# Scores in each group's own bank pair, and the small PE jobs last in each attention step

## The reference

```python
x = L0_attn_x                                             # (1, 2048, 128)
h = _layernorm(x)
Q, K, V = h @ Wq + bq, h @ Wk + bk, h @ Wv + bv           # 16 heads of 64
Qp, Kp = relu(Q), relu(K)
Qc, Qs, Kc, Ks = Qp * cos(t), Qp * sin(t), Kp * cos(t), Kp * sin(t)
# over tokens: S += k v^T, z += k (cos and sin parts)
num = Qc @ S_cos + Qs @ S_sin
den = max(Qc . z_cos + Qs . z_sin, 1e-6)
x = x + (num / den) @ Wo + bo
xf = _layernorm(x)
top_w, top_idx = top_k(xf @ gate_w, 2); top_w = softmax(top_w)
y = gelu(xf @ w1[e] + b1[e]) @ w2[e] + b2[e]              # for the two experts of a token
x = x + sum of y weighted by top_w
```

## Time and profile before

| | us |
|---|---|
| median of 3 runs | 374.67 |
| lowest and highest | 371.89, 378.90 |
| the profiled execution: its own time | 376.67 |
| its span, from the first to the last instruction | 374.8 |

### The profile page before, as it was taken

The page is one execution under the profiler, slowest core; times in us unless marked ns, Lnnn a source line. Parts: engine busy times, 40 slices in busy tenths (PEclk is TensorE's granted clock), DMA queues, the critical chain, the costliest instruction groups (busy, mean ns, idle before and its releaser), DMA issues.

```text
span 374.8 us, 14556 instructions
## 1 busy us (share of the span) xinstructions
PE 334.9 (89%) x5821; PEld 301.5 (80%) x5821; DVE 240.9 (64%) x837; ACT 171.5 (46%) x449; POOL 130.5 (35%) x130
## 2 busy tenths in 40 slices
PE   7998978999999999989989998898998999999910
PEld 6776967888798888879978887887888899999910
DVE  4889846648887745888855588876557544454415
ACT  3773432457433454733443663244334455555600
POOL 5022331203008820301872020274307775445430
PEclk9999988999999999999999999999999999999985
DMA  7940622233000100000110006113635676776138
GB/s 253 306 198 2 258 90 86 99 126 134 3 7 26 57 3 2 0 2 14 35 42 2 2 1 177 54 44 99 166 97 175 177 227 190 207 189 173 33 88 250
DMA packets 32786, 38.36 MB, mean 102 GB/s; under 512 B 6187, under 2 KB 25024, under 8 KB 31696
## 3 DMA queue, kind: packets, MB, share of 16 engines
q1 hardware_dynamic: 27248, 31.39, 27.1%
q0 software_dynamic: 2272, 4.46, 3.5%
q10 hardware_dynamic: 3200, 1.58, 1.4%
HBM read 22.40 MB, written 15.47 MB: 101 GB/s over the span
## 4 chain that ended last, share of the span: by engine, by line
PE 70%; DVE 14%; issue 6%; DMA 3%; POOL 3%; ACT 1%; SPq 1%; DVEq 0%; ACTq 0%; POOLq 0%
PE ps L1399 9%; PE ps L1384 8%; PE ps L1269 8%; PE ps L1196 7%; PE ps L1210 6%; PE ps L1076 5%; PE ps L1078 5%; PE ps L1077 5%; PE ps L1223 4%; PE ps L1173 3%; PE ps L1246 3%; PE ps L1123 2%; DVE vcs L729 2%; DVE vb L725 2%; DMA zin<-zbuf 2%
## 5 line engine op out<-in xcount | busy, mean ns | idle before, releaser
L620 ACT ACTIVATE os<-ps,rot 128x130 f32<-128x130 f32 x128 | 40.3, 366 | 81.7 <-PE ps L1223 81.7
L448 POOL TENSOR_TENSOR on<-tcs,rden 128x1024 f32<-128x1024 f32 x16 | 30.5, 1904 | 102.5 <-DVE rden L802 102.4
L655 ACT ACTIVATE hT<-ps,b1t 128x128 f32<-128x128 f32 x156 | 44.5, 368 | 40.3 <-PE ps L1384 40.3
L522 POOL DMA_INDIRECT zbuf<-z,tokens x39 | 37.9, 972 | 29.4 <-DVE z L1017 25.0
L1223 PE MATMUL ps<-vcs,am 64*64 64x65 f32 x1024 | 43.9, 232 | 2.0 <-issue 0.7
L1196 PE MATMUL ps<-vcs,kn 64*64 64x130 f32 x1024 | 44.5, 287 | 1.1 <-DVE tcs L792 0.5
L1399 PE MATMUL ps<-w_sb,hT 128*128 x312 | 43.1, 282 | 1.1 <-issue 0.6
L777 DVE TENSOR_TENSOR mid<-ps,state 128x260 f32<-128x260 f32 x64 | 26.7, 417 | 26.4 <-PE ps L1196 26.1
L1399 PEld LDWEIGHTS ps<-w_sb,hT 128*128 128x128 f32 x312 | 37.8, 192 | 2.4 <-issue 2.0
L725 DVE TENSOR_TENSOR vb<-ps,bv_all 128x512 f32<-128x512 f32 x32 | 22.0, 689 | 27.2 <-PE ps L1078 27.2
L1223 PEld LDWEIGHTS ps<-vcs,am 64*64 64x64 f32 x1024 | 33.0, 136 | 4.7 <-PE ps L1223 2.8
(11 more groups left out here) (126 smaller groups left out, 662.3 us busy)
## 6 DMA issues: line engine op xcount, KB each, us to landing
ybuf<-spare SPq DMA_DIRECT2D x8, 1152.0 KB, 5.0
w1b<-in_L_ffn_w SPq DMA_DIRECT2D x25, 256.0 KB, 2.7
spare<-in_L_ffn_w SPq DMA_DIRECT2D x14, 256.0 KB
yb<-ybuf SPq DMA_DIRECT2D x39, 72.0 KB, 2.4
w_sb<-in_L_ffn_w SPq DMA_DIRECT2D x8, 256.0 KB, 4.2
x_sb<-in_L_attn_x SPq DMA_DIRECT2D x4, 256.0 KB, 5.0
zin<-zbuf SPq DMA_DIRECT2D x4, 256.0 KB, 5.1
zin<-zbuf ACTq DMA_DIRECT2D x4, 256.0 KB, 5.7
```

The source lines that it names most:

```text
L522: pool.indirect_dma_start(zbuf, bass.IndirectOffsetOnAxis(ap=tokens[:, b:b + 1], axis=0), z[:, b % ZR, :], None, bounds_check=2 * T - 1, o ...
L620: last = act.activation(os[:, n % 2, :, q, :], ps[:, slot(n):slot(n) + 2, CS + q * VW:CS + q * VW + VW], ACT.Copy, scale=rot[:, 4 + q, c:c ...
L655: act.activation(hT[:, b % 2, f, :], ps[:, b % 2 * 2 + f // 2, f % 2 * P:f % 2 * P + P], ACT.Gelu, bias=b1t[:, b % XR, f:f + 1]).then_inc( ...
```

## The change

Scores of a group go into columns 260 to 387 of the group's own bank pair instead of banks 0 and 1. They are computed one group ahead instead of two, and DVE masks each group by itself, as the first thing in its step. The wait for a free bank pair moves from the key-value products to the scores, which are now the first to write there. Banks 0 and 1 become free for small jobs, which stand last in each PE step, in a new function `fill`: the transposes of K for chunks 1 to 3 (16 transposes of 64 rows in place of two times four of 128), whole turns of chunks 0, 1 and 2, the projections of chunks 0 and 1, `turn_y`, `gate`, `ranks`, the transposes of the next section's x, and the first two blocks of the next section. The fronts keep 14 blocks (16 in the first section), V in two banks in turn, K's transposes of chunk 0, the projection of chunk 2 and the turn and projection of chunk 3; blocks go through banks 4 to 7. ACT's copies and DVE's reads of all these move along. At the start of the experts some steps change places (`turn_y`, `gate`, the turn and projection of chunk 3 one place earlier or later).

```diff
+SCORES = 2 * CS
+V_AT = ({2: 0, 4: 1, 6: 2, 8: 3, 10: 4, 12: 5, 13: 6, 14: 7}, {2: 0, 3: 1, 5: 2, 6: 3, 8: 4, 9: 5, 11: 6, 12: 7})
+OPEN_AT = (14, 13)
+OT_AT, WO_AT, KEYS_0_AT = 6, 8, 10
+STATS_AFTER = 4
+YT_AT, GATE_AT, RANKS_AT, BEFORE_AT, TABLE_AT, TURN_X_AT = 0, 2, 4, 7, 11, 11
+KEYS_AT = {1: 1, 6: 2, 10: 3}
+TURN_AT = {8: 0, 13: 1, 16: 2}
+SUMS_AT = {9: 0, 14: 1}
...
             def scores(i, n):
...
-                if n >= 2:
-                    pe.wait_ge(am_ok, i * PAIRS + p)
...
+                if n >= 3:
+                    pe.wait_ge(tcs_ok, i * GROUPS + n - 2)
                 for q in range(2):
-                    of = 2 * g + q
-                    at = of % (PH // 2) * HT
+                    of, at = 2 * g + q, SCORES + q * HT
...
             def key_values(i, n):
...
-                if n >= 3:
-                    pe.wait_ge(tcs_ok, i * GROUPS + n - 2)
...
-            def group(i, n):
-
-                if n < GROUPS:
+            def group(i, n, tail):
+
+                if 1 <= n < GROUPS:
                     key_values(i, n)
                 if n >= 1:
                     from_state(i, n - 1, 0)
                     from_state(i, n - 1, 1)
                     within(i, n - 1, 0)
-                if n + 2 < GROUPS:
-                    scores(i, n + 2)
+                if n + 1 < GROUPS:
+                    scores(i, n + 1)
                 if n >= 1:
                     within(i, n - 1, 1)
+                fill(i, n, tail)
...
+            def masked(i, n):
+
+                c = n // NG
+                if n % NG == 0:
                     dve.wait_ge(pair_in[c], i * 16 + 16)
-                dve.wait_ge(sc_ps, i * PAIRS + p + 1)
...
+                dve.wait_ge(kv_ps, i * GROUPS + n + 1)
...
                 for n in range(GROUPS):
...
+                    masked(i, n)
                     half_state(i, n)
                     if n >= 2:
                         taken(i, n - 2)
                     whole_state(i, n)
-                    if n % 2 == 1 and n // 2 + 1 < PAIRS:
-                        masked(i, n // 2 + 1)
...
             def attention(i, tail):
+                fill(i, 0, tail)
+                fill(i, 1, tail)
                 for n in range(GROUPS):
+                    if n == GROUPS - 1 and i + 1 < NS:
+                        block(i + 1, 0)
+                        block(i + 1, 1)
                     sums_out(i, n)
...
+                    fill(i, n + 2, tail)
```

More of the change, by code:

```diff
@@ L572, in turn_out @@
-            def turn_out(i, c):
+            def turn_out(i, c, bank):
                 act.wait_ge(oT_ps, 2 * (i * SC + c) + 2)
                 for half, spots in ((0, slice(0, 4, 3)), (1, slice(1, 3))):
-                    act.activation(turned(c)[:, :, spots, :], ps[:, 6 + half, :].rearrange("p (g q l) -> p g q l", q=2, l=HT),
+                    act.activation(turned(c)[:, :, spots, :], ps[:, bank + half, :].rearrange("p (g q l) -> p g q l", q=2, l=HT),
                                    ACT.Copy).then_inc(oT_ok, 1)
-            def front(i, tail):
[L580 to L592, removed]
@@ new lines, in keys, with block @@
+            def keys(i, c, bank):
+                for r in range(2):
+                    act.wait_ge(kn_ps, i * K_JOBS + 2 * c + r + 1)
+                    act.activation(kn[:, c, :].rearrange("p (b r d) -> p b r d", r=2, d=DH)[:, :, r, :],
+                                   ps[:, bank + r, :].rearrange("p (b d) -> p b d", d=DH), ACT.Copy).then_inc(kn_ok, 1)
+            def block(i, j):
+                dst = (kT if j < NP else qT)[:, j % NP, :]
+                col = (NP if j < NP else 0) + j % NP
+                act.wait_ge(big_ps, i * QK_JOBS + j + 1)
+                act.activation(dst, ps[:, 4 + j % 4, :], ACT.Relu, bias=bcols[:, col:col + 1]).then_inc(big_ok, 1)
@@ L593, in front @@
+            def front(i, tail):
+                for j in range(2 if tail else 0, QK_JOBS):
+                    block(i, j)
                     if tail and j == OT_AT:
[L594 to L597, removed]
+                        turn_out(i - 1, SC - 1, 2)
+                    if j == KEYS_0_AT:
+                        keys(i, 0, 2)
             def y_turned(u, bank):
@@ L877, in shares, with places @@
                 dve.tensor_scalar(wts[:, 1, :], th[:, here], -0.5, 0.5, ALU.mult, ALU.add).then_inc(wts_ok, 1)
-            def places(u, bank=6, at=0):
+            def places(u, bank):
                 cs = UNITS[u][1]
@@ new lines, in block @@
+            def block(i, j):
+                if j == 0:
+                    pe.wait_ge(xThi_ok, i + 1)
+                    pe.wait_ge(xTlo_ok, i + 1)
+                    if i >= 1:
+                        pe.wait_ge(tcs_ok, i * GROUPS - 2)
+                if j == 2 and i >= 1:
+                    pe.wait_ge(tcs_ok, i * GROUPS - 1)
+                if j >= 4:
+                    pe.wait_ge(big_ok, i * QK_JOBS + j - 3)
+                if i == 0 and j == NP:
+                    pe.wait_ge(whi_ok, 3)
+                    pe.wait_ge(wlo_ok, 3)
+                w, b = 1 if j < NP else 0, j % NP
+                split3(ps[:, 4 + j % 4, :], (w_hi[w], w_lo[w]), (xT_hi, xT_lo),
+                       lambda t: t[:, b * P:(b + 1) * P], lambda t: t[:]).then_inc(big_ps, 1)
@@ new lines, in keys @@
+            def keys(i, c, bank):
+                for pr in range(NP):
+                    for r in range(2):
+                        rows = slice(HT * r, HT * r + HT)
+                        last = pe.transpose(ps[:, bank + r, pr * DH:pr * DH + DH], kT[rows, pr, c * P:(c + 1) * P],
+                                            ident[rows, rows])
+                        if pr == NP - 1:
+                            last.then_inc(kn_ps, 1)
+            def front(i, tail):
+                if tail:
+                    project(i - 1, SC - 2)
+                for j in range(2 if tail else 0, QK_JOBS):
+                    block(i, j)
+                    if j in V_AT[tail]:
+                        values(i, V_AT[tail][j])
+                    if tail and j == OT_AT:
+                        pe.wait_ge(tcs_ok, i * GROUPS)
+                        turn_out(i - 1, SC - 1, 2)
@@ L1277, in turn_y, with gate @@
                 last.then_inc(yT_ps, 1)
-            def gate(u, bank=7):
+            def gate(u, bank):
                 pe.wait_ge(yT_ok, u + 1)
```

369 lines of the change are left out of this document (169 added, 200 removed).

## The result

The changed kernel takes 416.73 us (median of four runs, 416.27 to 417.65), the kernel before 375.57 in the runs beside it. The ratio is 1.1135, with a 95% interval from 1.1046 to 1.1225: slower, near the forecast of 424 and inside its range. The ratio leaves out one of the four runs of the kernel before (378.90 us), which was in the slower of its two states, and so it lies a little above the quotient of the two medians, 1.1096. The profiled execution took 416.29 us, with a span of 414.5.

The account below looks back on a forecast made before the run. PE was taken to bound the kernel. The terms summed to +49.6 us on the profiled 376.67, 426.3; that execution being 2.0 us above the median, the forecast was 424 us against 374.67, range 400 to 452.

Parts of the forecast that it names:

- The wait at the scores: Mid-step in the attentions, PE waits for DVE's `taken` before scores: step 2.41 us instead of 1.56, 52 times, +44.2 us.
- ACT's copies ahead of the scaling: In attention steps with K's transposes or turns, two ACT copies delay the next group's scaling: 20 x 0.45, +9.0 us.
- The small jobs fill none of the wait: At each step's end, jobs stand behind the waiting scores, lie on the loop in full and fill none of 0.85 us.
- The start of the attentions: PE's 1.04 us idle at each attention's start is covered by work now inside the front: -4 us (0 to -4).
- Section 0's issue gaps: In section 0's attention, gaps of 4.3 us and the half clock behind them shrink: -3 us (0 to -7).
- The lost cover at the experts' start: Before the first expert block, projections no longer cover DVE and ACT: +3.7 us, and +1 for half speed afterwards.
- DVE's reading of the gate and the places: Moved from the front into steps 2 to 6 of three sections, delaying the next mask: +2 us (0 to 4).
- the transposes of K: Per chunk, two jobs of 0.36 us against one of 0.64, so cheaper: 16 x 0.08, -1.3 us.
- the first front: V in two banks and the split mask gain only in the first front: -2 us (0 to -3).
- The small jobs pay and the wait does not bind: Rival: `taken` reaches PE within 1.05 us, the attention step stays 1.56 us, about 367 us; chance 0.07.
- Half of it: Rival: DVE's and ACT's parts overlap better, the attention loop closes at 2.0 us, about 395 us; chance 0.07.
- The clock falls: Rival: gaps of 0.85 us in every 2.41 lower PE's clock part of the time, about 451 us; chance 0.12.

Follow-up runs that it names:

- Experiment 2: The changed kernel with the small PE jobs of steps 2 to 15 ahead of the scores instead of at the step's end: 382.81 us, ratio 1.0155.
- experiment 4: The kernel before with only one wait added, scores waiting for the `taken` that DVE makes in the same step: 394.37 us, ratio 1.0478.
- experiment 1: The changed kernel with DVE's mask third in its step, behind `half_state` and `taken`, instead of first: 406.52 us, ratio 1.0783.
- experiment 3: The changed kernel with ACT's copies of a job behind the scaling instead of ahead of it: 409.86 us, ratio 1.0873.
- Experiment 5: The changed kernel with ACT's last scaling of each section ahead of the last turn's copies and the next front's blocks 0 and 1: 409.74 us, ratio 1.0932.
- experiment 8: The changed kernel with jobs ahead of scores, mask third, ACT's last scaling first, and DVE's residual sum before the ones columns: 371.59 us, ratio 0.9887.

## Why the prediction was right, point by point

*The wait at the scores* is the cause, as the prediction put it. It predicted about 50 idle stretches of some 0.85 us released by `taken`; there are 51, of 0.81 in the mean. Experiment 2 undoes most of it by the place of the jobs, experiment 4 makes it in a kernel that has nothing else of the change, experiment 1 shortens it by DVE's order: each moved the time in the sense that the loop demands. Its size was put too high: +44.2 for the wait and +9.0 for ACT's copies are 53.2, and the line reads 41.2 us. The plain step is 2.25 us and not 2.41, chiefly since the next products follow `within` after 0.11 us. In the earlier trace rows there stood 0.24, but DVE's answer ended just before the products started, and that piece of the row very likely held a wait: in the same step of the kernel before, the other eight matmuls of `within` are followed by the scores after 0.11 us (118.74).

```profile
118.63 0.29 PE L1223 MATMUL ps<-vcs,am 64*64 64x65 f32 x8
```

So the 0.05 us that the prediction called spare were DVE's hand-over to PE, and the kernel before waited for DVE already there, though no list of waits shows it. The lesson lies in the reading: an interval between two starts is a cost only if nothing was awaited in it.

*ACT's copies ahead of the scaling*: +9.0 predicted. Taking them away behind the scaling (experiment 3, whose edit leaves the ends alone) gave back 6.9 us by the times and some 9.8 by the ratios, 5.0 of them in waits. The 20 long waits of the changed kernel are as many as the prediction counted, some 0.33 us longer than the others instead of 0.45: 6.6 us by that estimate, so the term was right in kind and somewhat large.

*The small jobs fill none of the wait*: right, and it decides the case. It is their place alone that costs 34 us (experiment 2).

*The start of the attentions*, -4: it came in three sections of four. The four waits of 1.04 us for `state` are gone in sections 1 to 3. In section 0 the wait became 1.37 us, behind one of 2.19 for V that is new. The total for `state` fell only from 5.1 to 3.6 us because the four waits at the sections' ends grew from 0.23 to 0.56 us each. So the term was worth about -3 in the later sections, and the start of section 0's attention took some 2.5 back (2.19, and 1.37 less 1.04).

```profile
31.40 0.68 PE L1193 MATMUL ps<-vcs,kn 64*64 64x130 f32 x16 [2.19 <-DVE vb L735]
...
33.45 0.47 PE L1207 MATMUL ps<-state,qT 64*64 64x130 f32 x8 [1.37 <-DVE state L785]
...
151.97 0.45 PE L1207 MATMUL ps<-state,qT 64*64 64x130 f32 x8 [0.56 <-DVE state L785]
```

*Section 0's issue gaps*, -3: they are gone from the waits, 4.3 us of them (2.73 and 1.60), and so are the shorter ones of the later sections. The half clock behind them is gone too, but others came (see the rivals).

*The lost cover at the experts' start*, +3.7 and +1: the gap is there, 5.0 us instead of about 4, and PE is slow behind it. The first block starts 6.74 us after the last `within` began; the prediction took 5.5, where its own rows give 266.34 - 260.52 = 5.82.

```profile
300.08 0.73 PE L1220 MATMUL ps<-vcs,am 64*64 64x65 f32 x16
...
301.38 0.44 PE L1308 MATMUL ps<-ident,yb 128*128 128x128 f32 x2
306.82 2.05 PE L1407 MATMUL ps<-spare 128*128 128x128 f32 x8 [5.00 <-DVE spare L1016]
308.66 2.70 PE L1257 MATMUL ps<-wo_sb,oT 128*128 128x128 f32 x16
```

The first expert block takes 2.05 us against 1.16, the projection 2.70. Experiment 5 puts 1.6 us of the gap down to ACT's order; what sets the other 3.4 was not tried.

*Not foreseen*: the 3.3 us for `x_sb`. The prediction moved the last group's scaling and sum against the front, but did not follow POOL's normalising to what would stand beside it on DVE.

*Not told apart*: DVE's reading of the gate and the places (+2), the transposes of K (-1.3) and the first front (-2) have no run of their own. The transposes' group is busy 11.8 us where it was 19.3, but such sums count overlapping instructions.

*The rivals.* "The small jobs pay and the wait does not bind" needed DVE's order to be another and `taken` to reach PE in time; with jobs and mask placed otherwise, and the two ends put right, experiment 8 comes near that kernel, at 371.6 us beside the 367 that the rival gave, though 18 waits are left in it. "Half of it", a loop of 2.0 us and 395, did not come: the plain step is 2.25. "The clock falls" came in small only. In the windows of the changed kernel (columns as in the earlier trace rows):

```profile
41.00:50.00 9.00, 6.93 (x272) 6.24 (x264) 5.23 (x17) 3.07 (x9) 3.94 (x4) 1.00 0.35 138
...
112.60:116.00 3.40, 2.77 (x68) 2.57 (x64) 2.90 (x17) 0.72 (x3) 0.00 (x0) 0.55 0.04 10
116.00:140.00 24.00, 17.94 (x559) 16.06 (x563) 12.70 (x41) 7.64 (x21) 14.92 (x14) 1.00 0.10 31
303.70:310.60 6.90, 3.78 (x19) 3.81 (x20) 2.98 (x9) 1.25 (x4) 2.43 (x3) 0.53 0.45 121
```

With PE busy 17.94 of 24 us (75%, where the prediction had near two thirds), idle 0.66 to 1.0 us in nearly every step, the granted clock is 1.00, the 2.4 GHz level. It stood at 0.50, the 1.2 GHz level, three times for some 3.3 us: from 34.1 behind the waits of 2.19 and 1.37, and from 112.3 and 259.1 inside the loop, each a step behind scores that had waited 1.06 us (at 109.80 and 257.36). The same wait in section 2 (183.83) had no such stretch behind it, so what set them is open. A fourth stretch, of about 7 us, began 1.6 us into the gap of 5.0 ahead of the experts and ran on behind it. The page of the Trainium skill that the prediction named, TensorE: Matmul & The Clock Gate, section "A second HAM failure mode: psum-queue depth-cycling", describes a loop that swings between both levels; such a loop over PSUM banks with a gap per round stands here, and in 51 steps with a gap the clock fell and came back twice: the trace bears the rule out in a small part only.

## What to carry to other kernels

When a buffer gets an earlier first writer, draw the loop from that writer through the other engines and back, and count what the writing engine can do before the wait, not what it has to do in all. Work that could fill the wait must stand ahead of the waiting instruction in its queue; behind it, it lengthens the loop and brings its copies along. Then order the other engines' steps by who is waited for: the sum that frees the buffer first, masks and copies for later use behind it.

## What the runs showed of the hardware

A DVE copy can stand still for about the whole length of a POOL instruction. In the changed kernel the 32 copies of 16 columns last 167 ns at least, 170 in the median and 1892 at most, with a mean of 329, which leaves room for three long ones: one in each of the three fronts where they meet POOL's normalising (1.92 us each).

```profile
L728 DVE COPY vcs<-cs x32: 167/170/1892, 11.4 to 233.5; 128x16 f32<-128x16 f32 x32
```

In the kernel of experiment 8, where the two do not meet, the longest of 32 is 183 ns, and in the kernel before 184. DVE's sums out of PSUM beside the same POOL instruction keep their 0.42 us (145.69 in the changed kernel, POOL from 144.53). This agrees with the Trainium skill, SBUF — State Buffer, section "SBUF: two separate sides", which says that the port pair shared by VectorE and GpSimd is an exclusive lock, held for a whole instruction, while the other engine blocks in full; on VectorE's side it names instructions in a two-port mode and those with two inputs in SBUF, and the sums have one of theirs in PSUM.
